# One exp over two scores: an attention loop whose PSUM banks are planned anew

## The reference, cut to what matters

```python
x = x + attention(x)          # x: (2, 1024, 128), 16 heads of 8 dimensions
x = layernorm(x)
x = layernorm(x + ffn(x))

# attention, scale = 1 / sqrt(16)
scores = einsum('bhqd,bhkd->bhqk', q, k) * scale
attn = softmax(scores, axis=-1)
out = einsum('bhqk,bhkd->bhqd', attn, v)        # then the projection wo, bo

# ffn, all weights fp32, hidden width 512
h = silu(x @ w1 * s1) * (x @ w2 * s2)
h = gelu(h @ h1 * t1); h = gelu(h @ h2 * t2)
y = h @ w3 * s3
```

## Time and profile before

| | us |
|---|---|
| median of 3 runs | 448.57 |
| lowest, highest | 448.32, 449.69 |
| the profiled execution | 449.5 |
| its span, first to last instruction | 447.8 |
| start of the first run's scores to the last run's | 40.5 to 317.5 |
| steps of four scores, to the last step's product | 320.6 to 352.6 |

### The profile page before, as it was taken

One profiled execution on the slowest core, in us unless ns is written; L12 is line 12 of the kernel. 1 busy time (PEld: TensorE's weight loads), 2 busy tenths in 40 slices (PEclk: granted clock), 3 DMA queues, 4 the chain that ended last, 5 costly groups with the idle time before them and its releaser, 6 DMA issues.

```text
span 447.8 us, 9355 instructions
## 1 busy us (share of the span) xinstructions
PE 432.3 (97%) x3498; PEld 237.3 (53%) x3498; DVE 374.1 (84%) x719; ACT 379.0 (85%) x727; POOL 95.8 (21%) x176
## 2 busy tenths in 40 slices
PE   8999989999999999999999999999999899999995
PEld 3544435454544545444445444545333488877884
DVE  5799979999999999999999999998884577647636
ACT  4497989999999989999999999999999976677762
POOL 9760200100000010000001002363311172036103
PEclk9999999999999999999999999999999999999999
DMA  5568850121131110213111111031022000000101
GB/s 150 170 216 144 300 168 27 48 85 40 48 121 48 31 45 21 57 48 113 55 34 44 38 39 47 12 48 30 27 33 55 10 13 2 1 1 1 47 2 49
DMA packets 18976, 27.67 MB, mean 62 GB/s; under 512 B 5680, under 2 KB 9520, under 8 KB 18544
## 3 DMA queue, kind: packets, MB, share of 16 engines
q1 hardware_dynamic: 18320, 26.44, 21.4%
q10 hardware_dynamic: 608, 0.59, 0.5%
HBM read 16.92 MB, written 8.52 MB: 57 GB/s over the span
## 4 chain that ended last, share of the span: by engine, by line
PE 80%; ACT 9%; SPq 3%; DVE 3%; DMA 2%; issue 2%; POOL 0%; POOLq 0%; DVEq 0%; ACTq 0%
PE ps L1491 25%; PE ps L1412 19%; PE ps L1601 15%; PE ps L1475 12%; ACT arena L738 4%; PE ps L1337 2%; DMA parts_q<-arena 2%; ACT hf L738 2%; PE ps L1348 1%; PE ps L1545 1%; DVE negmax L1079 1%; PE ps L1441 1%; PE ps L1377 1%; SPq L515 1%; SPq L488 1%
## 5 line engine op out<-in xcount | busy, mean ns | idle before, releaser
L1079 DVE TENSOR_REDUCE negmax<-ps 128x1 f32<-128x512 f32 x394 | 245.2, 683 | 17.0 <-PE ps L1412 15.6
L738 ACT ACTIVATE arena<-ps 128x512 f32<-128x512 f32 x360 | 190.7, 612 | 18.8 <-PE ps L1475 14.5
L1475 PE MATMUL ps<-qx,kx 64*128 64x512 f32 x512 | 172.5, 448 | 1.6 <-DMA qx<-mT 1.6
L1412 PE MATMUL ps<-kx,qx 61*128 61x512 f32 x436 | 146.1, 430 | 0.2 <-DVE negmax L1079 0.2
L1491 PE MATMUL ps<-arena,v_pad 128*32 128x256 f32 (+3 forms) x1328 | 105.3, 407 | 4.3 <-ACT arena L738 3.4
L1412 PEld LDWEIGHTS ps<-kx,qx 61*128 61x128 f32 x436 | 69.6, 185 | 68.6 <-DVE negmax L1079 47.3
L1475 PEld LDWEIGHTS ps<-qx,kx 64*128 64x128 f32 x512 | 80.3, 184 | 28.5 <-ACT arena L738 13.5
L738 ACT ACTIVATE hf<-ps 128x512 f32<-128x512 f32 x152 | 84.5, 632 | 4.1 <-PE ps L1475 4.0
L1601 PE MATMUL ps<-hid,w_high 128*128 128x512 f32 (+1 forms) x296 | 68.2, 388 | 0.8 <-issue 0.4
L1601 PEld LDWEIGHTS ps<-hid,w_high 128*128 128x128 f32 x296 | 54.2, 188 | 12.3 <-issue 0.8
L1491 PEld LDWEIGHTS ps<-arena,v_pad 128*32 128x32 f32 x1328 | 28.6, 108 | 39.4 <-issue 32.9
(11 more groups left out here) (116 smaller groups left out, 375.6 us busy)
## 6 DMA issues: line engine op xcount, KB each, us to landing
qx<-parts_q SPq DMA_DIRECT2D x60, 64.0 KB, 2.2
late_sb<-in_late SPq DMA_DIRECT2D x3, 1280.0 KB, 5.6
kx<-parts_k SPq DMA_DIRECT2D x56, 64.0 KB, 2.2
w_high<-parts_d SPq DMA_DIRECT2D x32, 64.0 KB, 2.2
parts_q<-prt SPq DMA_DIRECT2D x3, 512.0 KB, 6.6
parts_q<-arena SPq DMA_DIRECT2D x3, 512.0 KB, 7.4
xT_sb<-in_xT SPq DMA_DIRECT2D x4, 256.0 KB, 4.0
xT_sb<-arena SPq DMA_DIRECT2D x28, 32.0 KB
```

The costliest lines, as they stand in the source:

```text
L738: nc.scalar.activation(probs(n // HG)[:, heads(n), :], ps[:, PLAN["score", n][0], :], ACT.Exp, scale=SCALE).then_inc(exp_done, 1)
L1079: nc.vector.tensor_reduce(negmax[:, t // TURNS % 2, part, h * QT + q:h * QT + q + 1], ps[:, half_bank(p), :], AX.X, ALU.max, negate=True)\
L1412: nc.tensor.matmul(ps[:, half_bank(m), :], qx[at, slot, qc, h, q * P:(q + 1) * P], kd[slot][at, h, :] if part == APART else kx[at, slot, h ...
L1475: nc.tensor.matmul(ps[:, bank, :], kx[at, slot, h % PAIR, kt * P:(kt + 1) * P], qx[at, slot, qc, h % PAIR, :], start=True, stop=True)\
```

## The change

One ACTIVATE takes two scores of a run, where their banks lie side by side, and writes both to their places in SBUF. `exp` takes a tuple of one or two scores, waits for the later of them, reads banks `banks[0]` to `banks[-1]`, and adds two to `exp_done` at its end. The three places of four exps become twelve places of one tensor, `exps`, which reaches from the end of `attn` over the old `probs_2` to `hf`; `place_of` numbers them, and two exps of one instruction lie a fixed step apart.

`bank_plan` now also returns `EXPS`, which says for each run how its scores are grouped. Banks 0 and 1 are neighbours, and so are 6 and 7; of three banks in rotation two are neighbours, and they stand first or last in the order of the run. So a run has the form (pair, single) or (single, pair). A run of `TURN_AT` whose other two banks are neighbours, and a run that begins a unit with the pair first, keep three single exps. Of the 151 runs 93 are (single, pair), 43 are (pair, single), 14 have three single exps and one has no score; the two runs ahead of them are (pair, single). In the loop a score takes the bank of the score three before it, as before, or, after a change of the rotation, another of the same run. In the steps of four scores the pairs use banks 0 and 1 and banks 4 and 5: four banks in place of five, two exps a step, in the first such step three.

```diff
@@ -48,7 +48,8 @@
 QC = L // C
 ARENA = 16512
 SLOT_BYTES = 16384
-LATE_AT = ARENA + 6 * SLOT_BYTES + TOK * 4 + 3 * D * 4
+RING = 4
+LATE_AT = ARENA + 6 * SLOT_BYTES + RING * C * 4 + TOK * 4 + 3 * D * 4
 U_ALL = G_ALL * QC
 KT = L // P
 PARTS = 3
@@ -78,7 +79,7 @@
 TILES = C // P
 
 
-FIRST_BANKS, LATE_BANKS = [7, 0, 6, 1], (4, 5)
+FIRST_BANKS, LATE_BANKS = [0, 1, 7, 6], (4, 5)
 MAX_BANK = 2
 JOB_BANKS = [0, 1, 6, 7]
 STEPS_ALL = U_ALL * KT
@@ -134,8 +135,20 @@
 TURN_AT = {min((2 * TURNS * (w + 1) - 1 - AHEAD) // RUN + 3, RUNS + 1): w for w in range(1, U_ALL)}
 
 
+HEADS = (1, 0, 3, 2), (1, 3, 0, 2)
+
+
 def heads(n):
-    return ((1, 0, 3, 2), (1, 3, 0, 2))[n // HG >= TAIL][n % HG]
+    return HEADS[n // HG >= TAIL][n % HG]
+
+
+def place_of(n):
+
+    return n % (3 * HG) if n < TAIL * HG else ((n // HG - TAIL + TAIL % 3) % 2) * HG + n % HG
+
+
+def place_of_head(k, h):
+    return place_of(k * HG + HEADS[k >= TAIL].index(h))
 
 
 def scores_of(g):
@@ -170,39 +183,72 @@
 
 def bank_plan():
 
-    order, last, plan = FIRST_BANKS[:-1], {}, {}
-    held = FIRST_BANKS[-1]
-
-    def place(key):
-        bank = order.pop(0)
-        order.append(bank)
+
+    order, held = FIRST_BANKS[:3], FIRST_BANKS[3]
+    last, plan, exps = {}, {}, {}
+
+    def place(key, bank):
         plan[key] = bank, last.get(bank)
         last[bank] = key
 
-    place(("max", 0))
+    def beside(x):
+        return abs(order[x] - order[x + 1]) == 1
+
+    def pair(banks, ns, x):
+        if (banks[x] < banks[x + 1]) != (place_of(ns[x]) < place_of(ns[x + 1])):
+            banks[x:x + 2] = banks[x + 1], banks[x]
+
+    place(("max", 0), order[2])
     for g in range(-RUN_BEFORE, GROUPS_ALL):
-        if g in TURN_AT and g < RUNS:
-            place(("max", TURN_AT[g]))
-        for n in scores_of(g):
-            if n == TAIL * HG:
-                order[3:3] = LATE_BANKS
-                last.update({bank: ("reduced", 2 * U_ALL * TURNS) for bank in LATE_BANKS})
-            place(("score", n))
-        if g in TURN_AT and g >= RUNS:
-            place(("max", TURN_AT[g]))
-        w = unit_from(g)
+        ns, w = list(scores_of(g)), unit_from(g)
+        if g < RUNS:
+            alone = False
+            if g in TURN_AT:
+                place(("max", TURN_AT[g]), order[0])
+                alone = beside(0)
+                order = order[1:] + order[:1]
+            banks = list(order)
+            x = 0 if beside(0) else 1
+            if len(ns) < RUN or alone or (w and x == 0):
+                exps[g] = [(n,) for n in ns]
+            else:
+                pair(banks, ns, x)
+                exps[g] = [tuple(ns[0:2 - x]), tuple(ns[2 - x:])]
+            if alone:
+                order[0:2] = order[1], order[0]
+        else:
+            x = 0 if beside(0) else 1
+            spare = order[2 - 2 * x]
+            if g == RUNS:
+                last.update({bank: ("reduced", U_ALL * UNIT) for bank in LATE_BANKS})
+                banks = order[x:x + 2] + [spare, LATE_BANKS[0]]
+                exps[g] = [tuple(ns[0:2])] + [(n,) for n in ns[2:]]
+            else:
+                banks = order[x:x + 2] + list(LATE_BANKS)
+                exps[g] = [tuple(ns[0:2]), tuple(ns[2:4])] if ns else []
+                if ns:
+                    pair(banks, ns, 2)
+            if ns:
+                pair(banks, ns, 0)
+        for n, bank in zip(ns, banks):
+            place(("score", n), bank)
+        if g >= RUNS and g in TURN_AT:
+            place(("max", TURN_AT[g]), spare)
         if w == 0:
             plan["pv", w] = held, None
         elif w is not None:
-            place(("pv", w))
-            order.remove(plan["pv", w][0])
-            order.insert(0 if g >= RUNS else len(order), held)
+            bank = order[0] if g < RUNS else spare
+            place(("pv", w), bank)
+            order.remove(bank)
+            order.append(held)
             last[held] = ("unit", w - 1)
-            held = plan["pv", w][0]
-    return plan
-
-
-PLAN = bank_plan()
+            held = bank
+            if g >= RUNS and not beside(0) and not beside(1):
+                order[1:3] = order[2], order[1]
+    return plan, exps
+
+
+PLAN, EXPS = bank_plan()
 
 WO_BANK, X1T_BANK, INEXACT_BANK = [2, 3, 6, 7], [2, 3, 6, 7], 2
 GATE_BANKS, GELU_BANK = [(0, 2, 6), (0, 2, 4)], 4
@@ -265,7 +310,7 @@
             return ctx.enter_context(nc.semaphore(name))
 
 
-        arena = [sb(f"arena{n}", [P, PARTS * MT * TOK], BF16) for n in range(2)]
+        arena = [sb(f"arena{n}", [P, PARTS * MT * TOK + n * 2 * RING * C], BF16) for n in range(2)]
         xT_sb = sb("xT_sb", [P, TOK])
         wq_sb, wk_sb, wv_sb = (sb(f"w{n}_sb", [P, D]) for n in "qkv")
         wo_sb = wq_sb
@@ -302,7 +347,8 @@
         def over_sb(t):
             return attn[:, U_ALL - 4 + t % 4, :]
 
-        probs_2 = arena[1][:, 2 * U_ALL * C:].bitcast(F32).rearrange("p (s h c) -> p s h c", s=2, h=HG)
+        exps = arena[1][:, 2 * U_ALL * C:].bitcast(F32).rearrange("p (n c) -> p n c", c=C)
+        hf = exps[:, 2 * HG:2 * HG + RING, :]
 
         prt = sb("prt", [P, 4 * TOK], BF16)
         high = prt[:, 0:4 * TOK].bitcast(F32).rearrange("p (n t) -> p n t", n=2)
@@ -325,13 +371,6 @@
         mT = sb("mT", [P, 2, P])
 
         x1 = v_sb[:, :, :, :].rearrange("p g k e -> p (g k e)").rearrange("p (t d) -> p t d", d=D)
-        hf = sb("hf", [P, RING, C])
-
-        def probs(k):
-
-            if k >= TAIL:
-                return probs_2[:, (k - TAIL) % 2]
-            return hf if k % 3 == 2 else probs_2[:, k % 3]
 
         nonzero = hf[:, :, :].rearrange("p n c -> p (n c)").bitcast(BF16)\
             .rearrange("p (n c) -> p n c", c=HID)
@@ -732,11 +771,13 @@
                 nc.scalar.activation(part[name][0][:, c * C:(c + 1) * C].bitcast(F32R), proj[:, n, :],
                                      ACT.Copy).then_inc(split_high, 1)
 
-            def exp(n):
-
-                act.wait_ge(scores, n + 1)
-                nc.scalar.activation(probs(n // HG)[:, heads(n), :], ps[:, PLAN["score", n][0], :], ACT.Exp,
-                                     scale=SCALE).then_inc(exp_done, 1)
+            def exp(ns):
+
+                act.wait_ge(scores, ns[-1] + 1)
+                banks, places = (sorted(of) for of in ([PLAN["score", n][0] for n in ns], [place_of(n) for n in ns]))
+                step = places[-1] - places[0] or 1
+                nc.scalar.activation(exps[:, places[0]:places[-1] + 1:step, :], ps[:, banks[0]:banks[-1] + 1, :],
+                                     ACT.Exp, scale=SCALE).then_inc(exp_done, len(ns))
 
             attn_flat = arena[1][:, 0:2 * U_ALL * C].bitcast(F32)
 
@@ -778,9 +819,9 @@
                     late_unit = unit_to(g - 1)
                 else:
                     late_unit = None
-                for n in scores_of(g):
-                    exp(n)
-                    if g >= RUNS and n % HG == 1:
+                for ns in EXPS[g]:
+                    exp(ns)
+                    if g >= RUNS and ns[-1] % HG == 1:
                         if late_unit is not None:
                             copy_unit(late_unit)
                         if g in TURN_AT:
@@ -1489,7 +1530,7 @@
                         bank_free(PLAN["pv", w][1])
                 for n in range(HG):
                     ins = nc.tensor.matmul(ps[32 * n:32 * n + 32, PLAN["pv", w][0], c0:c1],
-                                           v_pad[:, w // QC % 2, kt, n, :], probs(k)[:, n, c0:c1],
+                                           v_pad[:, w // QC % 2, kt, n, :], exps[:, place_of_head(k, n), c0:c1],
                                            start=(kt == 0 and c0 == 0), stop=(kt == KT - 1 and c1 == C),
                                            tile_position=(0, 32 * n))
                 if c1 == C:
```

1 line of the change is left out of this document (removed).

## The result

| | before | after |
|---|---|---|
| median, us | 449.13 | 471.39 |
| profiled execution, us | 449.5 | 471.4 |
| its span, us | 447.8 | 469.7 |
| loop, start of run 0 to start of run 149 | 276.95 | 296.20 |
| steps of four scores to the feed-forward part | 32.03 | 33.88 |

(The median before is that of the runs taken beside the changed kernel. One of the six executions of a later experiment, with pairs in the steps alone, ran at a granted clock of 0.66 and took 542.66 us; it is left out, and all figures are of the others.) The ratio is 1.0492, 95% interval 1.0464 to 1.0521: 22 us slower, and outside the range.

The account below looks back on a forecast made before the run. The prediction took TensorE, with ScalarE's lateness on top, to bound the loop. It summed +2.8 (first 128 runs), -1.3 (21 later runs) and +0.3 (steps of four scores) to +1.8 us, 450.4 us on the median; range 443 to 458.

Parts of the forecast that it names:

- The way round: Loop's paired runs: pair's first score to the next score waiting for its bank takes 1.79 us, over TensorE's 1.69.
- to the exp's start 0.06: Paired runs of the loop: the pair's exp starts 0.06 us after its second score ends.
- start of the pair's first score to end of its second, 0.67 us: Paired runs of the loop: the pair's two scores span 0.67 us when the first has waited.
- The sign of being wrong that the prediction gave last: Paired runs: an unnamed wait, such as a half waiting for VectorE between a pair's scores, enters the way; no size.
- a rival too, at 1.85 to 1.86: Paired runs of the loop: scores spanning 0.73 or an exp of 1.08 us make the way longer; 459 us, chance 0.22.
- The third rival, 473: Pair's exp: reading across two banks costs as two instructions, 1.19 us, way 1.97; +25 us, 473 us, chance 0.03.
- What the pair saves ScalarE: ScalarE's exps: a pair holds the engine 0.90 us against 0.97 for two singles, saving 0.07 us a pair.
- A copy then spills only 0.08 us: Loop: a 0.485 us copy on ScalarE spills about 0.08 us into the next pair; backlog gone by the next run.
- The runs with the weight roundings: The 21 later runs, 40.79 us before, with nine weight roundings on ScalarE: 39.3 plus 0.2 us, so -1.3 us.
- The steps of four scores: Stage after the loop, two pairs a step: +0.05 us in each of eight steps with an output projection; +0.3 us.
- Two banks fewer rotate (four in place of five), and this costs nothing but those 0.4: Steps of four scores: rotating four banks costs only the 0.4 us of the eight steps with an output projection.
- Costed at nothing: Feed-forward part, score order, products, DMA issues and VectorE's halves: taken to add no time.

Follow-up runs that it names:

- run 149: No follow-up kernel: a numbered run of the kernel's own loop; from the start of run 0 to its start took 276.95 us before, 296.20 after.
- no half between: The changed kernel with TensorE's order edited so that no half stands between the two scores of a pair in paired runs; 459.72 us, ratio 1.0223.
- alternating rows: The changed kernel with halves and scores alternating array rows one by one in place of two by two, a half still between a pair's scores; 473.31 us, ratio 1.0523.
- back to back: The kernel with alternating rows, with halves moved so that TensorE gets a pair's two scores directly one after the other; 452.20 us, ratio 1.0059.

## Why the prediction was wrong, point by point

**The bound.** Right: TensorE's loop with ScalarE's lateness on top. The lateness was a small prize: with the pairs' exps cut to three quarters, 32 runs still took 57.21 us, 1.2 less than before. One reading under it was not what it seemed: that two more stretches repeat the 58.41 us within 0.01 came from windows of that length. By the starts of the runs they take 58.37 and 58.70.

**The way round: the mechanism right, the step from the second score to the exp mis-sized.** The step that failed is "to the exp's start 0.06". From the recorded end of the pair's second score to the exp it measured 0.10 us with both scores in the same rows and 0.29 with different rows, 0.18 in the mean. The step before it, "start of the pair's first score to end of its second, 0.67 us", held by the record: 0.66 in the mean, 0.73 and 0.57. Together that is 0.843 in place of 0.73. The rest of the sum was good: the exp 1.024 for 1.01, the release 0.053 for 0.05. In all 1.92 for 1.79, and 0.13 in 136 paired runs makes 17.7 of the 21 us by which 450.4 missed. This is an estimate, as it lets every paired run pay the same; those of the table at the end of the experiments don't.

Two things were wrong in the 0.06. It was read from a single exp behind its own score (106.04 to 106.11), whose wait is part of the exp; a pair has an instruction for its wait and starts 0.082 us behind the count in place of 0.022. This alone is 0.06 us of the 0.11. And it was laid behind the score's recorded end, though ScalarE waits for its count, which comes after that of the half before it in the list. The earlier trace rows had this in it already: the third score's record ends at 69.93, but it is counted at 70.047, behind its half at 70.012. From 69.26 that makes 0.787 us, and with 0.082 on top 0.87, as in the changed kernel. No exp showed it there, since ScalarE had exps of other scores ahead of it and took this one up at 70.29. A matmul's end is modelled, so the record alone doesn't say when a matmul is really through; the sums from start to start don't depend on it.

The sign of being wrong that the prediction gave last, a half that puts itself between the two scores of a pair, came near: the half does, though by its place in the list and not by waiting for VectorE. The chain was on the page as a rival too, at 1.85 to 1.86, with 0.73 for the scores and a chance of 0.22. Its 0.73 is just what pairs in the same rows show. What it lacked is the same 0.06. The third rival, 473, came nearest the time, and that is luck: across two banks the exp takes no surcharge (1.025 us, not 1.19).

**Beside the way round.** Two kinds of run lost more than was counted. In the first 128 runs the 12 that begin a unit went from 2.12 to 2.38 us each, and the 12 ahead of transposed maxima from 1.91 to 2.17, together +6.3 us; the 12 with the maxima gained 0.13 each.

**The Trainium skill's figure.** By the Trainium skill ("ScalarE: Activation LUTs", section "What ACT_TABLE_LOAD costs") the pair would, as an estimate from its 186 ns plus 0.833 ns a column, have lasted 1.04 us. The rows gave 1.01, and 1.025 was measured, in the middle. The slope agrees from 512 to 1024 columns (0.82 to 0.83), where the prediction had one duration, 597 ns, which can't show a slope.

**What the pair saves ScalarE.** I had 0.07 us. From the start of a pair to that of the single exp behind it are 0.92 us (the row at 105.78: 1.51 less the 0.59 of the single exp), two singles back to back issue in 0.954 (0.477 each). So 0.034 us, 1 us in 32 runs. Even at no cost the change had little to give.

**The copies.** "A copy then spills only 0.08 us" held: a run with a relu copy, such as that from 122.81, takes 1.94 us like its neighbours. The backlog is gone as I said; what replaced it was larger.

**The runs with the weight roundings.** Forecast -1.3, measured +2.3: 19 x 0.13 = 2.5 of the difference of 3.6 is the same term. The base of 40.79 us was 0.27 too long (40.52 by the starts of the runs).

**The steps of four scores.** Forecast +0.3, measured +1.85. The time of two successive steps after, TensorE, then ScalarE:

```profile
345.83 0.73 PE L1516 MATMUL ps<-qx,kx 64*128 64x512 f32 x4
...
347.91 1.04 PE L1516 MATMUL ps<-qx,kx 64*128 64x512 f32 x4
...
350.30 0.73 PE L1516 MATMUL ps<-qx,kx 64*128 64x512 f32 x4
```

```profile
346.46 4.03 ACT L779 ACTIVATE arena<-ps 128x1024 f32<-128x1024 f32 x4 [1.07 <-PE ps L1516]
350.92 1.94 ACT L779 ACTIVATE arena<-ps 128x1024 f32<-128x1024 f32 x2 [0.44 <-PE ps L1516]
```

Steps take 2.08 and 2.39 in turn. The pair starts 0.63 after its scores, not 0.56, and the next issues 0.92 behind it, not 0.90, so the third score is held until 0.54 behind the first. But single exps on the same four banks took as long (34.07), with steps of 2.08 and 2.42 in turn, and on the old five banks these steps take 2.08 each. "Two banks fewer rotate (four in place of five), and this costs nothing but those 0.4" was the step that failed here: the old five banks are worth 2 us there, whichever way the exps are grouped.

**Costed at nothing.** The feed-forward part (95.2 against 95.1), the new places, the new rotation in the loop and VectorE (TensorE's halves waited 47.6 us for it, before 47.3) were rightly left out. The separate instruction for a pair's wait was not in the sum at all. If single and pair could start alike, 0.06 us in 136 paired runs would be some 8 us, an estimate from the 0.082 and the 0.022; no run tried it.

## What to carry to other kernels

When one instruction takes over the work of two, write down how long it holds each buffer, from the first producer's start to the release, before counting the fixed cost that it saves: a loop with as many buffers as it fills in a run can't go faster than that way round, however idle its engines are. Then look at what stands in the producer's list between the two fills, since the consumer waits for that foreign instruction too: the counts come in the order of the list. Make the sum to the time of the semaphore's count, not to the recorded end of the producer, and from the count on with an instruction of the kind that will wait there.

## What the runs showed of the hardware that was not expected

An ACTIVATE may read two PSUM banks side by side without a surcharge: 0.602, 0.813, 0.919 and 1.025 us at 512, 768, 896 and 1024 columns, 0.82 to 0.83 ns a column throughout. The count that frees both banks comes 0.01 us behind its end (121.312 and 121.322).

TensorE's halves and scores are counted in the order of its list, also when they lie in different rows and the later one's record ends first: 888 of 888 in each of five traces (before, after, no half between, alternating rows, back to back), at least 0.034 us apart. In the kernel with alternating rows, where an unrelated half is counted between the two scores of a pair, the second's count comes 0.24 us behind its recorded end in the mean, and the kernel with the halves moved was 21 us faster.

A pair's exp waits in an instruction of its own and starts 0.082 us behind the count, a single exp 0.022.

When both scores of a pair start together and nothing stands between them, the exp begins 0.13 us after their recorded end (0.64 after their start): 0.015 to the first count, 0.034 to the second, 0.083 to the exp.

A score that was held up for 0.15 us (119.32 to 119.47), and so came apart from the half beside it, made its run 0.24 us longer than the 1.69 of a run without a wait.
